# A four-layer cross-attention stack on one core: input and gate products of batch 0 begin inside the norm before the state space block; keys and values move into the wait for the decay rows

## What is computed

```python
def _mamba2_block(x, norm_w, in_proj_w, conv_w, conv_b, dt_bias, A_log, D_skip, gnorm_w, out_proj_w):
    zxbcdt = _rms(x, norm_w) @ in_proj_w
    z = zxbcdt[..., :D_INNER]
    xBC = zxbcdt[..., D_INNER:D_INNER + CONV_DIM]
    dt = jax.nn.softplus(zxbcdt[..., -H_M:] + dt_bias)
    padded = jnp.pad(xBC, ((0, 0), (D_CONV - 1, 0), (0, 0)))
    conv = conv_b + sum((padded[:, k:k + L, :] * conv_w[:, k] for k in range(D_CONV)))
    xBC = jax.nn.silu(conv)
    ...
    def step(h, inp):
        dec, u, bt, ct = inp
        h = h * dec[:, :, None, None] + u[..., None] * bt[:, None, None, :]
        ...
    y = ys.transpose(1, 0, 2, 3) + D_skip[None, None, :, None] * xh
    u = _rms(y.reshape(b, L, D_INNER) * jax.nn.silu(z), gnorm_w)
    return resid + u @ out_proj_w
```

## Time and profile before

| | us |
|---|---|
| three runs | 987.97, 991.68, 993.81 |
| median | 991.68 |
| the profiled execution, whole | 989.22 |
| span of its core, first to last instruction | 987.4 |
| TensorE busy in the span | 871.0 (88%) |
| VectorE / ScalarE busy | 525.5 / 450.8 |

### The profile page before, as it was taken

One profiled execution on the slowest core, in us unless ns is written; L12 is line 12 of the kernel. 1 busy time (PEld: TensorE's weight loads), 2 busy tenths in 40 slices (PEclk: granted clock), 3 DMA queues, 4 the chain that ended last, 5 costly groups with the idle time before them and its releaser, 6 DMA issues.

```text
span 987.4 us, 10846 instructions
## 1 busy us (share of the span) xinstructions
PE 871.0 (88%) x4450; PEld 406.0 (41%) x4452; DVE 525.5 (53%) x714; ACT 450.8 (46%) x686; POOL 46.4 (5%) x39
## 2 busy tenths in 40 slices
PE   3986799989999999967899999989688998889987
PEld 2533344443434444525224436234245443554342
DVE  2367999932333012144744326358729676794542
ACT  3564222264243315343343341736677367753524
POOL 0000000020000000000300000000002000220000
PEclk9899899998979999987799797999689999899999
DMA  9000000000000000030000000000000000000011
GB/s 376 20 1 0 1 0 0 0 1 1 1 1 1 0 1 0 1 126 1 1 1 1 1 1 2 1 1 0 1 0 2 1 0 0 2 1 1 2 43 43
DMA packets 3006, 15.63 MB, mean 16 GB/s; under 512 B 656, under 2 KB 912, under 8 KB 2320
## 3 DMA queue, kind: packets, MB, share of 16 engines
q1 hardware_dynamic: 2816, 12.88, 3.3%
q0 software_dynamic: 144, 2.10, 0.5%
HBM read 12.87 MB, written 2.10 MB: 15 GB/s over the span
## 4 chain that ended last, share of the span: by engine, by line
PE 68%; DVE 18%; ACT 10%; issue 2%; DMA 1%; DVEq 0%; SPq 0%; POOL 0%; ACTq 0%
PE ps L405 66%; DVE VB L632 3%; ACT AR L619 3%; DVE AR L2082 1%; DVE AR L2172 1%; DMA CX<-in_ctxT 1%; DVE AR L2179 1%; DVE AR L2175 1%; DVE AR L503 1%; DVE AR L1955 1%; DVE AR L2167 1%; DVE VB L1820 1%; PE ps L578 1%; DVE AR L1817 1%; DVE AR L644 1%
## 5 line engine op out<-in xcount | busy, mean ns | idle before, releaser
L405 PE MATMUL ps<-AR,WA 128*128 128x512 f32 (+3 forms) x780 | 340.4, 597 | 11.7 <-DVE AR L2181 3.6
L405 PEld LDWEIGHTS ps<-AR,WA 128*128 128x128 f32 (+2 forms) x780 | 143.6, 190 | 195.2 <-issue 182.6
L405 PE MATMUL ps<-AR,CN 128*128 128x512 f32 (+3 forms) x320 | 117.3, 630 | 11.4 <-DVE AR L498 6.2
L405 PE MATMUL ps<-AR 128*64 128x128 f32 (+5 forms) x680 | 102.5, 420 | 10.0 <-ACT AR L1691 5.0
L405 PEld LDWEIGHTS ps<-AR 128*64 128x64 f32 (+4 forms) x680 | 54.3, 168 | 50.5 <-issue 17.4
L644 DVE TENSOR_TENSOR AR<-ps,AR 128x512 f32<-128x512 f32 x24 | 16.6, 692 | 106.3 <-ACT AR L624 106.3
L619 ACT ACTIVATE AR<-ps 77x2048 f32<-77x2048 f32 x24 | 44.2, 1870 | 58.9 <-PE ps L405 58.9
L405 PEld LDWEIGHTS ps<-AR,CN 128*128 128x128 f32 (+2 forms) x320 | 40.6, 169 | 65.2 <-issue 40.9
L632 DVE TENSOR_REDUCE VB<-ps 128x16 f32<-128x1232 f32 x32 | 44.7, 1438 | 33.5 <-PE ps L405 33.5
L2082 DVE SCALAR_TENSOR_TENSOR AR<-AR,VC 128x512 f32<-128x512 f32 x72 | 50.6, 748 | 7.0 <-ACT AR L1637 6.0
L405 PE MATMUL ps<-KB,WA 128*128 128x512 f32 (+1 forms) x120 | 52.6, 608 | 1.3 <-ACT AR L1675 1.0
(11 more groups left out here) (313 smaller groups left out, 1087.0 us busy)
## 6 DMA issues: line engine op xcount, KB each, us to landing
WA<-in_m SPq DMA_DIRECT2D x1, 2856.0 KB, 9.6
WA<-in_m SPq DMA_DIRECT2D x1, 2560.0 KB, 15.8
X<-in_xT POOLq DMA_DIRECT2D x1, 2048.0 KB, 9.5
WA<-in_m SPq DMA_DIRECT2D x1, 2048.0 KB, 20.7
out<-X SPq DMA_DIRECT2D x4, 512.0 KB, 3.1
WB<-in_m SPq DMA_DIRECT2D x1, 1024.0 KB, 22.6
AR<-in_rows SPq DMA_DIRECT2D x1, 640.0 KB, 10.2
WA<-in_m SPq DMA_DIRECT2D x1, 512.0 KB, 16.5
```

Of the source, the lines that this page charges most:

```text
L405: return nc.tensor.matmul(out, lhsT, rhs, start=first, stop=last)
```

## The change

The norm of the second half becomes pieces "xm" (means, squares) and "xq" (mean square, roots) inside the "in" pieces of batch 0; the squares of "nb" become a piece "sq", and "nb" itself comes after the sixth product. The gates of batch 0 follow directly on its six products, ahead of "dt", and are no longer in the "gate" place behind "ef". The keys and values stand at the head of "rows". Products of batch 0 use other banks of PSUM (`inbank`), and the keys move from banks 6 and 7 to banks 0 and 1. In the first step of the first half the state, which is zero, isn't scaled, and VectorE copies the new state instead of adding it; in the first step of the second half the scaling comes after the exponentials of both batches.

```diff
@@ mamba_order
                     for k in range(XBC):
                         yield "in", b, j, k
-                        if (j, b, k) == (0, 0, 1):
-                            yield "nb", 0, 0, 0
+                        if (j, b) == (0, 0) and k in (0, 1, 3, 5):
+                            yield {0: "xm", 1: "xq", 3: "sq", 5: "nb"}[k], 0, 0, 0
...
                     if (j, b) == (0, 0):
+                        yield "gate", 0, 0, 0
                         yield "dt", 0, 0, 0
...
-                    yield "gate", b, j, 0
+                    if j or b:
+                        yield "gate", b, j, 0
...
+        def inbank(b, j, k):
+
+            return bank(b, (k + 2) % 4 if (j, b) == (0, 0) else k % 4)
@@ TensorE
             output2(1)
-            for b in BS:
-                pe.wait_ge(*after("o2", nk(1, 4, 2 * b + 1)))
-            norm_pe(pe, "x3", 1, ST, True)
...
             pe.wait_ge(*after("ra_ln", B))
-            keys_pe(pe, "a3", w("Wk3", 2))
-            values_pe(pe, "a3", w("Wv3", 2))
...
+                elif piece == "xm":
+                    for u in BS:
+                        pe.wait_ge(*after("norm_sum", CENTRED["x3"] + B + u + 1))
+                        mm(bank(1, u), cn("mean"), ST[u][:, 0, :]).then_inc(sem("norm_mean"), 1)
+                elif piece == "xq":
+                    for u in BS:
+                        pe.wait_ge(*after("norm_sqs", NORMS["x3"] + B + u + 1))
+                        mm(bank(1, u), cn("mean"), ST[u][:, 0, :]).then_inc(sem("norm_ms"), 1)
...
                 elif piece == "rows":
+                    pe.wait_ge(*after(of("iev", 0), 10))
+                    keys_pe(pe, "a3", w("Wk3", 2))
+                    values_pe(pe, "a3", w("Wv3", 2))
                     pe.wait_ge(sem("rows"), 1)
...
                     for k in range(XBC, XBC + 4):
-                        pe.wait_ge(*after(of("ef", b), 2 * j + (1 if k < XBC + 2 else 2)))
+                        if j or b:
+                            pe.wait_ge(*after(of("ef", b), 2 * j + (1 if k < XBC + 2 else 2)))
+                        else:
+                            pe.wait_ge(*after(of("iev", b), k - 3))
@@ ScalarE
                 elif piece == "rows":
+                    prep_act(act, "a3")
                     act.wait_ge(sem("rows_mm"), 1)
...
+                    if j == 0 and b:
+                        convolved(0)
                     for c in range(4):
                         act.wait_ge(*after(of("in_mm", b), 10 * j + XBC + c + 1))
-                        nc.scalar.activation(ZF[b][:, c, :], bank(b, (XBC + c) % 4), ACT.Silu).then_inc(sem(of("iev", b)), 1)
...
-                    if b:
+                        nc.scalar.activation(ZF[b][:, c, :], inbank(b, j, XBC + c), ACT.Silu).then_inc(sem(of("iev", b)), 1)
+                    if j or b:
+                        convolved(b)
+                    if b or j == 0:
                         nc.scalar.preload_act_table_set("natural_log_exp_and_others")
...
+                    if s:
+                        decay(b)
                     act.wait_ge(*after(of("xt_mm", b), n + 1))
...
+                    if s == 0 and j and b:
+                        for u in BS:
+                            decay(u)
@@ VectorE
-                    dve.wait_ge(*after(of("se", b), n + 1))
                     dve.wait_ge(*after(of("s_new", b), n + 1))
-                    TT(STATE[b], SE[b], bank(b, 0), ALU.add).then_inc(sem(of("s7", b)), 1)
+                    if n:
+                        dve.wait_ge(*after(of("se", b), n))
+                        TT(STATE[b], SE[b], bank(b, 0), ALU.add).then_inc(sem(of("s7", b)), 1)
+                    else:
+                        nc.vector.tensor_copy(STATE[b], bank(b, 0)).then_inc(sem(of("s7", b)), 1)
```

More of the change, by code:

```diff
@@ L1225, in _ @@
                         pe.wait_ge(*after("ra_xn", 2))
+                        pe.wait_ge(*after("norm_ln", NORMS["x3"] + B * J))
                     if k == 2 and j == 0 and b == 0:
-                        pe.wait_ge(*after("kv_vs", LAYER["a3"] + 1))
+                        pe.wait_ge(*after("o2", nk(1, 4, 1)))
+                    elif k == 2 and j == 0:
+                        pe.wait_ge(*after("norm_ln", NORMS["r3"] + B))
                     if k == 3 and j and b == 0:
@@ L1289, in _ @@
                     pe.wait_ge(*after("ab", j + 1))
-                    pe.wait_ge(*after(of("iev", b), 10 * j + 6))
+                    pe.wait_ge(*after(of("iev", b), 10 * j + (6 if j or b else 10)))
+                    if j == 0 and b == 0:
+                        pe.wait_ge(*after("kv_kb", KEYS["a3"] + 2))
+                        pe.wait_ge(*after("kv_vs", LAYER["a3"] + 1))
                     if j == 0 and b:
@@ L1613, in _ @@
             attn_act(act, "a2", 1, table=False, meanwhile=first_roots)
-            norm_act(act, "x3", 1, None, ST, "eps5", True, XC, table=False)
-            prep_act(act, "a3")
-            act.wait_ge(*after("x3", 4 * J))
-            for b in BS:
-                nc.scalar.activation(SQ7[b], X[:, :, b, T:2 * T], ACT.Square).then_inc(sem("norm_sq"), 1)
             for piece, b, j, s in mamba_order():
@@ L1676, in _, with decay @@
                 elif piece == "s1":
-                    if n:
+                    def decay(b):
                         act.wait_ge(*after(of("s7", b), n))
-                    else:
-                        act.wait_ge(sem("m0"), B)
-                    for h in range(HM):
-                        head = slice(h * PD, (h + 1) * PD)
-                        col = 32 * (B * j + b) + h
-                        ins = nc.scalar.activation(SE[b][:, head], STATE[b][:, head], ACT.Copy, scale=EEN[:, s, col:col + 1])
-                    ins.then_inc(sem(of("se", b)), 1)
+                        for h in range(HM):
+                            head = slice(h * PD, (h + 1) * PD)
+                            col = 32 * (B * j + b) + h
+                            ins = nc.scalar.activation(SE[b][:, head], STATE[b][:, head], ACT.Copy, scale=EEN[:, s, col:col + 1])
+                        ins.then_inc(sem(of("se", b)), 1)
+                    if s:
+                        decay(b)
                     act.wait_ge(*after(of("xt_mm", b), n + 1))
```

48 lines of the change are left out of this document (30 added, 18 removed).

## The result

| | us |
|---|---|
| kernel before, four runs | 986.72 to 993.81, median 989.83 |
| changed kernel, four runs | 973.63 to 979.88, median 976.63 |
| ratio | 0.986, 95% interval 0.9835 to 0.9886 |
| profiled execution of the changed kernel | 977.36, span 975.5 |

The change saves 13.2 us by the medians, 1.3%, and 1.4% by the ratio; the forecast was 11.1 us and a median of 980.5, range 975 to 987. On the chip of a later measurement the same file gave 0.9873 (0.9849 to 0.9897). Lines have moved: L2082 is now L2119, L2141 L2178, L1661 L1689, L1675 L1709, L1666 L1701, L1671 L1705, L2172 L2211 and, for the first step's copy, L2213.

What follows compares the result with a forecast made beforehand. TensorE, 88% busy, was taken to lose time idling behind VectorE and ScalarE, then at half clock. Gains of 9.3 + 1.8 = 11.1 us from 989.22 give 978.1; with 2.46 us to the median, 980.5 was forecast, range 975 to 987.

Steps and rivals of the forecast that it cites:

- Start of the block: Norm copies move to where ScalarE has room, so VectorE goes straight from the last sum into the convolution, 1.5 us earlier.
- rival 4: Roots or "dt" come late, VectorE's chain waits and the head start does nothing: 991.5 at worst; chance 0.06.
- Two table loads hidden: ScalarE's two extra table loads around batch 0's gate Silu, 1.28 us each, stay off the path with 2.2 us cover.
- Keys and values in the wait: Key and value products fill TensorE's idle stretch before the transposes and keep its clock up: L1661 4.55 us earlier.
- Gates end 8.4 us earlier: Only batch 1's gates remain behind the exponentials, ending at 715.9 against 724.33, with 2.85 us lost to half clock.
- State products 10.35: First state products start at 722.2, 10.35 us earlier, as one ScalarE scaling ahead of them is gone.
- first step 9.3: End of the first state step 9.3 us earlier, allowing 1 us more of half clock there.
- Second half: First state scaling leaves the path of batch 0's exponential: 1.8 us gained, bounds 0 and 3.5.
- Sum 11.1: Whole-kernel gain: 9.3 us at the end of the first step plus 1.8 in the second half.
- 1 (clock stays up): Full clock holds between selection and state steps: 16.4 us gained, 975; chance 0.13.
- 2 (clock falls earlier): Half clock already at the transposes and selection, L1661 only 1.5 us earlier: 4 us gained, 987.5; chance 0.14.
- 3, half clock in several state steps: Half clock lasts into the state steps, about 8 us per step; two steps give 996.5; chance 0.03.

Runs made afterwards that it cites:

- e3: Changed kernel with batch 0's gates back at their old place behind its exponentials, and two table loads fewer; 983.25 us, ratio 0.992.
- e1: Changed kernel with the last attention's key and value products cut to 8 columns, most keys and values left out; 981.54 us, ratio 0.9923.
- e4: Kernel before with only the last attention's keys and values moved between batch 1's input products and the transposes; 989.03 us, ratio 0.9988.
- e2: Changed kernel with state scalings and the addition as before, each step scaling the state first; 983.08 us, ratio 0.992.
- e5: Kernel before with only the scalings changed: first step copies the state, second half scales it behind batch 1's exponential; 986.95 us, ratio 0.9974.
- e6: Changed kernel with batch 1's decay products and exponentials ahead of batch 0's in the first half; 979.02 us, ratio 0.9888.
- a0_again: The changed kernel measured once more without any edit; 978.06 us, ratio 0.9873.
- e10: e6 with the unread products of e9, without the two behind the first exponential; 970.16 us, ratio 0.9795.
- e9: Changed kernel with unread TensorE products, sized to fit, in waits at the selection, decays, transposes and state products, in both halves; 973.77 us, ratio 0.9829.
- e7: Changed kernel with 11 unread TensorE products: seven behind the selection, four behind batch 0's first decay exponential; 981.06 us, ratio 0.992.
- e11: e6 with one more unread product, in the second half's wait ahead of batch 1's decay products; 976.96 us, ratio 0.9861.

## Why the prediction was right

The forecast held in its mechanism and nearly in each term. By its own steps, with 2.44 us taken off each time after:

- **Start of the block, 1.5 us.** Right: L2119 at 671.97 (674.41 - 2.44) against 671.9 forecast, 1.47 earlier. The roots made it, there is no idle row ahead of L2175 or L2178 (1.47 earlier too), so rival 4 did not come. The margins are as thin as forecast: the roots are done 0.2 us ahead of L2175 (677.78 + 0.63 against 678.64), the "dt" products 0.9 us ahead of L2178 (683.65 + 0.60 against 685.14). e3 has the same position without the gates in front, so the norm's rearrangement gives this alone.
- **Two table loads hidden, cover 2.2 us.** Right: 2.31 us of idleness are left behind the second. The Trainium skill (ScalarE: Activation LUTs, What ACT_TABLE_LOAD costs) has a drain of 1.38 us on top of 1.28; the trace after disagrees again: the load starts at 678.42, as L1672 ends at 677.78 + 0.63, and the next instruction starts at 679.72, 1.30 us on.
- **Keys and values in the wait, L1661 4.55 us earlier.** 4.1: right. The clock stayed at 1.00 to 704. e1 shows that they work through the clock, and e4 that alone they are worth almost nothing.
- **Gates end 8.4 us earlier.** 8.0: right, with 2.7 us lost to half clock (9.83 for 7.1), where I took 2.85.
- **State products 10.35, first step 9.3.** 9.85 and 10.0. The half clock in the first step was 3.4 us and not longer than before, as I had allowed.
- **Second half, 1.8 us, bounds 0 and 3.5.** Under-sized, within its bounds: by the profile it is 2.8 (L2211 of step two of batch 0, before 857.14, after 846.80: 12.8 earlier in all, less 10.0). e2 gives 6.1 - 2.2 - 1.7 = 2.2. Both are more than the one scaling that the forecast took off the path (2.02 us).
- **Sum 11.1.** The terms to here make 12.8. The 1.6 us up to 14.3 come from the half clock at 957.8 that is no longer there. No step had it. It is in no other profile of the study, those of e4 and e5 included, which leave most of the change out, so I don't count it to the change. The ratios of the two measurements, 0.986 and 0.9873, are 13.9 and 12.6 us.
- **Rivals.** 1 (clock stays up) and 2 (clock falls earlier) did not come, the clock fell again in the wait ahead of the decays; 3, half clock in several state steps, in no kernel of the study lasted beyond the first. The Trainium skill (TensorE: Matmul & The Clock Gate, The HAM clock gate) says that full clock returns only after a sustained busy stretch and at a point that varies. The trace agrees: the gates ran from 708.96 on without a wait, and at half clock until 714.2.

What the prediction did not see is that the terms don't add. Taken out of the changed kernel one by one, the parts cost 3.2 (e1), 6.1 (e2) and 6.6 us (e3), 15.9 in all and without the start's 1.5; put into the kernel before, two of them gave 0 and 2.6 up to the last attention. Most of the difference is half clock at the second half's gates, 1.7 us in six of the twelve experiments and in neither of the two kernels compared. Leave these 1.7 us out, and two parts have the same price both ways: keys and values 1.5 us taken out (3.2 - 1.7) and 1.5 put in (-0.15 + 1.7), the scalings 4.4 and 4.3. So what does not add in these two parts is the clock. That the changed kernel kept its clock there, with waits no shorter than e6's, is luck of position and not a merit of the change, though a0_again repeats it; the kernel before had the same luck (7.13 us), so their ratio does not rest on it. What puts a wait on the wrong side I can't say from these runs.

## What to carry to other kernels

Where TensorE is the bound but waits in places, read the granted clock beside every wait. Where the clock falls in it, a wait costs its own length and then half of the time of the work that follows at 0.50; moving independent products into it can be worth both. Where none are left, unread products of the right size did it here, beyond the noise in e10 and by the profile in e9. Size them by rows of the trace, since fill that is longer than the wait costs at once (e7).

A saving of 1 to 3 us ahead of such waits can vanish at another place. Compare positions from a common instruction ahead of the change, stretch by stretch, before you call an edit useless.

## What was not expected of the hardware

- The same two groups of small products with waits of 0.89 and 0.19 us are followed by full clock in some kernels and by half clock in others, and one product of 0.86 us in the first of the waits decided it (e6 against e11: 8.83 and 7.13 us, one profile each).
- Work that nobody reads made the kernel faster: 20 rows of it (8 + 8 + 2 + 2) took e6's order from 979.02 to 970.16 us, on two chips whose kernels before had medians of 989.68 and 991.64.
- Executions of one and the same kernel differ by their clock: of the six of e3_old_gates the two shortest (979.36 and 982.22 us) had a mean granted clock of 0.943 and 0.942, the other four (983.17 to 985.45) 0.933.
